# A four-layer graph network on one core: in the six SAGE rounds, a pair's gathered rows are transposed in front of the units of the pair ahead, and GpSimd scatters before it gathers

## The chip, the cores and the metric

The kernel runs on one core of one Trainium2 chip. The metric is the time on the device in microseconds. Of the kernel before there are three runs, and one more execution that was profiled.

## The reference

There are N = 100,000 nodes with 128 float32 features each and 50,000 edges (`src`, `dst`), sorted by `dst`. The destinations are drawn as the square of a uniform number, so they crowd at low node numbers: few nodes per edge at first, many later. Four layers follow each other, each with a residual and a layer norm.

```python
def _sage_conv(x, src, dst, W_l, b_l, W_r, n_nodes):           # layer 0, twice
    agg = jax.ops.segment_sum(x[src], dst, num_segments=n_nodes)
    cnt = jax.ops.segment_sum(jnp.ones((src.shape[0],), x.dtype), dst, num_segments=n_nodes)
    mean = agg / jnp.maximum(cnt, 1.0)[:, None]
    out = mean @ W_l + b_l + x @ W_r
    norm = jnp.linalg.norm(out, axis=-1, keepdims=True)
    return out / jnp.maximum(norm, 1e-12)                       # then relu
def sage_conv(h, W_l, W_r, bias):                               # layer 1, four times
    agg = jax.ops.segment_sum(h[src], dst, num_segments=n) * inv_deg[:, None]
    return jax.nn.relu(agg @ W_l + h @ W_r + bias)
...
x = _layernorm(x + _L0_gnn_ref(...), axis=-1)
x = _layernorm(x + _L1_gnn_ref(...), axis=-1)
x = _layernorm(x + _L2_gnn_ref(...), axis=-1)    # a graph attention layer
x = _layernorm(x + _L3_gnn_ref(...), axis=-1)    # a transformer layer with edge features
```

## The kernel before, in words

The kernel makes eight rounds over all edges and nodes and an output pass. Rounds 0 to 5 are SAGE rounds: rounds 0 and 1 are layer 0 (each with a division by the row's norm, round 1 with the residual and layer norm as well), rounds 2 to 5 are layer 1 (relu alone, round 5 with residual and layer norm). Round 6 is the attention layer (GAT), round 7 the transformer layer (TR). The change touches the SAGE rounds alone.

**Edges.** They are cut into 98 blocks of 512, and two blocks (q = 0 and 1) make a pair, so that a round has 49 pairs. For a block of a SAGE round:

- GpSimd gathers its source rows with 4 indirect DMAs of 128 rows each into `gath[q]` (`gathers`, L609), once DVE has put the block's source indices into `g_idx[q]` (`next_gather`, L1345, which waits until the last gathers with these indices have landed).
- PE transposes them into the bank `pe_bank[q]` (printed as edge_bank; L768) and raises `gt_ready[q]`.
- DVE runs one scan over 512 edges (L1363), which sums the rows of edges with one destination into `run[q]`, and copies the block's destination indices to `s_idx[q]` (`next_scatter`, L1351). The scan needs the last column of the scan before, so scans are serial.
- PE multiplies `run[q]` by W_l (L774) into `pe_bank[2 + q]`; ACT scales the rows by the inverse degree into `y_rows[q]` (L943) and raises `y_ready[q]`.
- GpSimd scatters y_rows with 4 indirect DMAs into `agg` in HBM (`scatters`, L618), where rows that are no end of a run go out of bounds and are left out.

**Nodes.** They are cut into 97 units of 1,024 (two groups s of 512) and a tail. For each unit SP loads the rows (`h_in`, L533) and the aggregates (`agg_in`, L539); PE transposes the rows (`front`, L856); ACT copies them to `h_t` (L1016); PE adds the bias (L862) and the product with W_r (L865) into `o_bank`; DVE adds the aggregates (`total`, L1521); ACT or DVE make relu or norms and ACT stores the rows. PE and ACT work one unit ahead (`front(u + 1)` in `unit(u)`).

**The order.** Each engine runs its own program in its own order, and semaphores tie them together. On PE, DVE, ACT and SP `schedule` sets it: for each pair i first `edge_pair(i)`, then the units whose last edges lie in the pairs before i. The number of units behind a pair comes from a table (`unit_end`) that the kernel works out from the edges: in a SAGE round 8 pairs have none, 11 have one, 13 have two, 11 three, 5 four, and behind the last pair come the remaining eight. SP waits ahead of the units of pair i for the scatters of the pairs before i. GpSimd has no units. Its loop of a SAGE round is the gathers of pair i+1 (both q), then the scatters of pair i (both q), with a wait in front of each. The attention and transformer rounds (`STAGGERED`) have another loop, which stays.

## Time and profile before

| | |
|---|---|
| median of 3 runs | 17478.66 us (17463.14 to 17509.43) |
| the profiled execution | 17477.8 us, its span 17476.0 us |
| rounds 0 to 5 (SAGE) | from about 1920 to 11900 us |
| attention round, transformer round | to about 14500, to about 16750 us |
| busy share of the span | PE 52%, DVE 42%, POOL 43%, ACT 29% |
| granted TensorE clock | 0.666 of 2.4 GHz, mean over the span |

The busy share is that of an engine over the whole span. In the rows further down, a time in front is the start in us from the span's start, the next number is how long the group of instructions was busy, and what stands in brackets at the end is the time for which that engine had been idle and what ended the wait: an instruction, a DMA, "issue" where nothing that the profile shows was waited for, or "remote" where the trace has no event near the end of the wait that could have released it. POOL is GpSimd, SPq and ACTq are the DMA issues of SP and ACT.

### The profile page before, as it was taken

What the parts mean: (1) busy time and instruction counts of PE and PEld (TensorE: products, weight loads), DVE (VectorE), ACT (ScalarE), POOL (GpSimd) and SP (SyncE); (2) the same over time, 40 slices, a digit from 0 to 9 for tenths busy, and PEclk for the clock granted to TensorE, in tenths of its full rate; (3) what the DMA queues carried; (4) which work ended last, traced back from release to release, by engine and by line L of the source; (5) the groups of instructions that cost most, each with busy time, mean ns of one, the idle gap of its engine ahead of it and who ended that gap; (6) DMA issues with size and microseconds to landing.
All of it is one profiled execution on the core that took longest, in us unless ns stands there. A gap on an engine that the chain in (4) does not pass through costs nothing. (4 is left out here: it accounts for less than half of the span.)

```text
span 17476.0 us, 215795 instructions
## 1 busy us (share of the span) xinstructions
PE 9144.7 (52%) x39289; PEld 6376.8 (36%) x39290; DVE 7406.0 (42%) x20909; ACT 5025.3 (29%) x11680; POOL 7457.3 (43%) x7460
## 2 busy tenths in 40 slices
PE   3664345534444455455545544554444446777765
PEld 1121234433333344344434434443333333444444
DVE  3664234424444112111111213446777774444456
ACT  0000022223443122122212213334555552222247
POOL 0546554354322654554365455433333326554410
PEclk9776566656665667666656765666666666677776
DMA  5000134524443245334424534554333332233457
GB/s 244 1 3 1 49 113 139 159 78 124 135 137 112 87 137 163 94 120 151 151 84 138 164 95 137 160 177 144 114 111 112 115 107 59 70 95 111 123 181 246
DMA packets 1168748, 2071.10 MB, mean 119 GB/s; under 512 B 283745, under 2 KB 292466, under 8 KB 1155794
## 3 DMA queue, kind: packets, MB, share of 16 engines
q1 hardware_dynamic: 662400, 1128.29, 21.5%
q10 hardware_dynamic: 267958, 563.32, 8.3%
q0 software_dynamic: 238336, 378.92, 8.0%
q14 instruction: 38, 0.31, 0.0%
q8 instruction: 16, 0.26, 0.0%
HBM read 1358.91 MB, written 772.63 MB: 122 GB/s over the span
## 5 line engine op out<-in xcount | busy, mean ns | idle before, releaser
L618 POOL DMA_INDIRECT agg<-y_rows,s_idx x3136 | 3229.8, 1030 | 2746.4 <-DVE s_idx L1351 1380.1
L862 PE MATMUL o_bank<-b_parts,ones_parts 3*128 3x512 bf16 (+1 forms) x1568 | 826.1, 527 | 4435.1 <-ACT h_t L1016 2314.9
L865 PE MATMUL o_bank<-w_r,h_t 128*128 128x128 f32 x12544 | 2804.2, 393 | 0.0
L865 PEld LDWEIGHTS o_bank<-w_r,h_t 128*128 128x128 f32 x12544 | 2394.9, 285 | 577.0 <-issue 576.1
L1521 DVE TENSOR_TENSOR total<-o_bank,agg_in 128x512 f32<-128x512 f32 (+1 forms) x1568 | 1042.7, 688 | 3353.4 <-DMA agg_in<-agg 2032.6
L609 POOL DMA_INDIRECT gath<-node_a,g_idx x1176 | 1130.7, 961 | 2414.4 <-DVE g_idx L1345 1174.7
L1016 ACT ACTIVATE h_t<-ht_bank 128x512 f32<-128x512 f32 (+1 forms) x1568 | 881.5, 593 | 3995.6 <-remote 2661.3
L862 PEld LDWEIGHTS o_bank<-b_parts,ones_parts 3*128 3x128 bf16 (+1 forms) x1568 | 150.4, 96 | 4816.2 <-ACT h_t L1016 2952.6
L609 POOL DMA_INDIRECT gath<-node_x,g_idx x784 | 785.6, 1002 | 1502.4 <-PE edge_bank L808 629.0
L943 ACT ACTIVATE y_rows<-edge_bank,inv 128x128 f32<-128x128 f32 x2352 | 671.5, 370 | 2609.7 <-remote 1039.6
L774 PE MATMUL edge_bank<-w_l,run 128*128 128x128 f32 x4704 | 903.3, 358 | 944.9 <-DVE run L1363 884.3
L1363 DVE TENSOR_TENSOR_SCAN run<-keep,run,edge_bank 128x512 f32<-128x512 f32 (+1 forms) x588 | 752.5, 1280 | 1201.9 <-PE edge_bank L768 570.2
L856 PE MATMUL ht_bank<-ident,h_in 128*128 128x128 f32 x6272 | 1125.2, 337 | 220.7 <-issue 113.2
L597 POOL DMA_INDIRECT rec_dram<-rec_rows,place_idx x784 | 755.4, 963 | 1121.4 <-DVE rec_rows L1302 896.5
L774 PEld LDWEIGHTS edge_bank<-w_l,run 128*128 128x128 f32 x4704 | 798.3, 259 | 1066.2 <-DVE run L1363 999.5
L1082 ACT ACTIVATE h_out<-t,small 128x128 f32<-128x128 f32 x2744 | 1102.6, 486 | 208.6 <-DVE small L1510 155.6
L609 POOL DMA_INDIRECT gath<-node_b,g_idx x784 | 786.2, 1003 | 799.7 <-PE edge_bank L768 414.3
L856 PEld LDWEIGHTS ht_bank<-ident,h_in 128*128 128x128 f32 x6272 | 976.2, 181 | 378.7 <-issue 282.0
L1526 DVE TENSOR_REDUCE small<-zeros 128x4 f32<-128x512 f32 x392 | 262.3, 684 | 1088.2 <-ACT zeros L1028 643.7
L768 PE MATMUL edge_bank<-ident,gath 128*128 128x128 f32 x2352 | 468.1, 359 | 460.7 <-DMA gath<-node_a,g_idx 216.1
L736 PE MATMUL edge_bank<-keep,rest_ones 128*128 128x512 bf16 (+1 forms) x784 | 336.1, 429 | 595.2 <-DVE place_f L1291 373.2
L609 POOL DMA_INDIRECT gath<-in_x_dram,g_idx x392 | 374.1, 954 | 634.8 <-DVE g_idx L1345 296.7
(249 smaller groups left out, 14550.0 us busy)
## 6 DMA issues: line engine op xcount, KB each, us to landing
agg_in<-agg SPq DMA_DIRECT2D x1560, 256.0 KB
node_a<-h_out ACTq DMA_DIRECT2D x780, 256.0 KB
h_in<-node_a SPq DMA_DIRECT2D x780, 256.0 KB
node_x<-h_out ACTq DMA_DIRECT2D x390, 256.0 KB
h_in<-node_x SPq DMA_DIRECT2D x390, 256.0 KB
node_b<-h_out ACTq DMA_DIRECT2D x390, 256.0 KB
h_in<-node_b SPq DMA_DIRECT2D x390, 256.0 KB
agg<-zeros ACTq DMA_DIRECT2D x96, 1024.0 KB
```

Source lines behind the costliest of these rows:

```text
L597: pool.indirect_dma_start(rec_dram[n], bass.IndirectOffsetOnAxis(place_idx[q][:, k:k + 1], 0), rec_rows[q][:, k, :], None).then_inc(rec_ou ...
L609: pool.indirect_dma_start(gath[q][:, k, :], None, h_of, bass.IndirectOffsetOnAxis(g_idx[q][:, k:k + 1], 0)).then_inc(gathered[q], 16)
L618: pool.indirect_dma_start(agg[order(r)], bass.IndirectOffsetOnAxis(s_idx[q][:, k:k + 1], 0), y_rows[q][:, k, :], None, bounds_check=N - 1, ...
L774: last = pe.matmul(pe_bank[2 + q][:, k * P:(k + 1) * P], run[q][:, k * P:(k + 1) * P], w_l[r][:], start=True, stop=True, skip_group_check= ...
L856: last = pe.transpose(ht_bank[s][:, j * P:j * P + p], h_in[s][0:p, j, :], ident[0:p, 0:p])
L862: pe.matmul(o_bank[s][0:p, :], ones_parts[:, 0:p], b_parts[:, r, :].unsqueeze(1).to_broadcast([3, RPP, P]), start=True, stop=False, skip_g ...
L865: last = pe.matmul(o_bank[s][0:p, j * P:(j + 1) * P], h_t[s][:, j, 0:p], w_r[r][:], start=False, stop=j == RPP - 1, skip_group_check=True)
L943: last = act.activation(y_rows[q][:, k, :], pe_bank[2 + q][:, k * P:(k + 1) * P], ACT.Copy, scale=inv[:, bass.ds(2 * i + q, 1), k])
L1016: act.activation(h_t[s][:, :, 0:p], ht_bank[s][:].rearrange("p (j n) -> p j n", j=RPP)[:, :, 0:p], ACT.Copy).then_inc(ht_ready[s], 1)
L1082: last = act.activation(h_out[s][0:p, j, :], of[s][0:p, j, :], ACT.Identity, scale=small2[0:p, 2 + 2 * turn, s * RPP + j:s * RPP + j + 1], ...
L1363: dve.tensor_tensor_scan(run[q][:], keep_of(i, q), pe_bank[q][:], run[1 - q][:, BLOCK - 1:BLOCK], ALU.mult, ALU.add).then_inc(run_ready[q], 1)
L1521: dve.tensor_tensor(flat(total[s], p), o_bank[s][0:p, :], flat(agg_in[s], p), ALU.add).then_inc(sum_ready[s], 1)
```

## The change

In the SAGE rounds three programs are written in another order.

- **PE.** The transposes of a pair (`sage_turn`) are taken out of `sage_pair`. Those of pair 0 come ahead of the schedule, behind `front(0)`; those of pair i+1 come right behind the W_l matmuls of pair i, so in front of the units of pair i.
- **DVE.** The copies of gather indices for the pair behind the next (`next_gather`) come behind both scans of pair i instead of in front of each, and wait for the gathers of pair i+1; two of them come ahead of the schedule.
- **GpSimd.** The gathers of two pairs come first; then the loop is scatters of pair i, gathers of pair i+2; the last two steps are scatters alone.

```diff
--- before.py
+++ after.py
@@ -645,23 +645,16 @@
                         for q in range(2):
                             next_scatters(q, n)
                     continue
-                with pool.Fori(0, PAIRS - 1) as i:
-
-                    for step, q in ((gathers, 0), (gathers, 1), (scatters, 0), (scatters, 1)):
-                        if step == gathers:
-
-                            pool.wait_ge(gt_ready[q], gt_ready.at(r, i + 1))
-                            pool.wait_ge(gidx_ready[q], gidx_ready.at(r, i + 2))
-                        else:
-
-                            pool.wait_ge(sidx_ready[q], sidx_ready.at(r, i + 1))
-                            pool.wait_ge(y_ready[q], y_ready.at(r, i + 1))
-                        pool.sem_inc(pool_turn, 1)
-                        step(q)
                 for q in range(2):
-                    pool.wait_ge(sidx_ready[q], sidx_ready.at(r, PAIRS))
-                    pool.wait_ge(y_ready[q], y_ready.at(r, PAIRS))
-                    scatters(q)
+                    next_gathers(q, 2)
+                with pool.Fori(0, PAIRS - 2) as i:
+                    for q in range(2):
+                        next_scatters(q, i + 1)
+                    for q in range(2):
+                        next_gathers(q, i + 3)
+                for n in (PAIRS - 1, PAIRS):
+                    for q in range(2):
+                        next_scatters(q, n)
 
 
         @block.tensor
@@ -760,13 +753,14 @@
             for r in range(NR):
                 kind, tail = ROUNDS[r][0:2]
 
+                def sage_turn(i, q, r=r):
+                    pe.wait_ge(gathered[q], gathered.at(r, i + 1))
+                    pe.wait_ge(run_ready[q], run_ready.at(r, i))
+                    for k in range(CPB):
+                        last = pe.transpose(pe_bank[q][:, k * P:(k + 1) * P], gath[q][:, k, :], ident[:])
+                    last.then_inc(gt_ready[q], 1)
+
                 def sage_pair(i, r=r):
-                    for q in range(2):
-                        pe.wait_ge(gathered[q], gathered.at(r, i + 1))
-                        pe.wait_ge(run_ready[q], run_ready.at(r, i))
-                        for k in range(CPB):
-                            last = pe.transpose(pe_bank[q][:, k * P:(k + 1) * P], gath[q][:, k, :], ident[:])
-                        last.then_inc(gt_ready[q], 1)
                     for q in range(2):
                         pe.wait_ge(run_ready[q], run_ready.at(r, i + 1))
                         pe.wait_ge(y_ready[q], y_ready.at(r, i))
@@ -774,6 +768,9 @@
                             last = pe.matmul(pe_bank[2 + q][:, k * P:(k + 1) * P], run[q][:, k * P:(k + 1) * P],
                                              w_l[r][:], start=True, stop=True, skip_group_check=True)
                         last.then_inc(yp_ready[q], 1)
+                    if not (isinstance(i, int) and i == PAIRS - 1):
+                        for q in range(2):
+                            sage_turn(i + 1, q)
 
 
 
@@ -888,6 +885,9 @@
                     tr_score(0, 0)
                     tr_values(0, 0)
                 front(0)
+                if kind == SAGE:
+                    for q in range(2):
+                        sage_turn(0, q)
                 schedule(pe, r, {SAGE: sage_pair, GAT: gat_pair, TR: tr_pair}[kind], lambda i: None, unit)
 
 
@@ -1356,13 +1356,15 @@
 
                 def sage_pair(i, r=r):
                     for q in range(2):
-                        next_gather(i, q, r)
                         dve.wait_ge(gt_ready[q], gt_ready.at(r, i + 1))
                         dve.wait_ge(yp_ready[q], yp_ready.at(r, i))
                         dve.wait_ge(run_ready[1 - q], run_ready.at(r, i + q))
                         dve.tensor_tensor_scan(run[q][:], keep_of(i, q), pe_bank[q][:], run[1 - q][:, BLOCK - 1:BLOCK],
                                                ALU.mult, ALU.add).then_inc(run_ready[q], 1)
                         next_scatter(i, q, r)
+                    if not (isinstance(i, int) and i == PAIRS - 1):
+                        for q in range(2):
+                            next_gather(i + 1, q, r)
 
                 def maxima(i, q, r, st, logits):
 
@@ -1583,6 +1585,9 @@
                             dve.bn_stats(place, ht_bank[s][:].rearrange("p (j n) -> p j n", j=RPP)[:, :, 0:p]).then_inc(bn_ready[s], 1)
                     st.end()
 
+                if kind == SAGE:
+                    for q in range(2):
+                        next_gather(0, q, r)
                 if kind == GAT:
                     gat_first()
                 if kind == TR:
```

PE, from the end of unit 0's front in round 0 to the head of its pair loop, before. `gath` are the gathered rows, `run` the scanned sums, and the load of `unit_end` is where the units of the pair begin:

```order
L865 MATMUL o_bank<-w_r,h_t 128x128 x4
L389 UNCONDITIONAL_BRANCH
L389 ISA
L768 MATMUL edge_bank<-ident,gath 128x128 x8
L771 REGISTER_ALU
L774 MATMUL edge_bank<-w_l,run 128x128 x8
L392 ISA
L392 TENSOR_LOAD unit_end
```

And the same stretch of the changed kernel:

```order
L862 MATMUL o_bank<-w_r,h_t 128x128 x4
L760 MATMUL edge_bank<-ident,gath 128x128 x8
L389 UNCONDITIONAL_BRANCH
L389 ISA
L766 REGISTER_ALU
L768 MATMUL edge_bank<-w_l,run 128x128 x8
L757 REGISTER_ALU
L760 MATMUL edge_bank<-ident,gath 128x128 x8
L392 ISA
L392 TENSOR_LOAD unit_end
```

The transposes with `gath` stood ahead of the matmuls with `w_l` in the loop; now they stand behind them, ahead of the units, and once in front of the loop.

GpSimd's loop of round 0 before, with the semaphores that each row waits for (`agg` is the table in HBM that is scattered to):

```order
L654 REGISTER_ALU [waits gt_ready0]
L609 DMA gath<-in_x_dram,g_idx 128x128 [waits gidx_ready0]
L609 DMA gath<-in_x_dram,g_idx 128x128 x3
L609 DMA gath<-in_x_dram,g_idx 128x128 [waits gt_ready1,gidx_ready1]
L609 DMA gath<-in_x_dram,g_idx 128x128 x3
L618 DMA agg<-y_rows,s_idx 100000x128 [waits sidx_ready0,y_ready0]
L618 DMA agg<-y_rows,s_idx 100000x128 x3
L618 DMA agg<-y_rows,s_idx 100000x128 [waits sidx_ready1,y_ready1]
L618 DMA agg<-y_rows,s_idx 100000x128 x3
L648 REGISTER_ALU
L648 COMPARE_AND_BRANCH
```

The same loop of the changed kernel:

```order
L618 DMA agg<-y_rows,s_idx 100000x128 [waits sidx_ready0,y_ready0]
L618 DMA agg<-y_rows,s_idx 100000x128 x3
L618 DMA agg<-y_rows,s_idx 100000x128 [waits sidx_ready1,y_ready1]
L618 DMA agg<-y_rows,s_idx 100000x128 x3
L622 REGISTER_ALU
L623 REGISTER_ALU [waits gt_ready0]
L609 DMA gath<-in_x_dram,g_idx 128x128 [waits gidx_ready0]
L609 DMA gath<-in_x_dram,g_idx 128x128 x3
L609 DMA gath<-in_x_dram,g_idx 128x128 [waits gt_ready1,gidx_ready1]
L609 DMA gath<-in_x_dram,g_idx 128x128 x3
L650 REGISTER_ALU
L650 COMPARE_AND_BRANCH
```

The gathers, which had their two waits for `gt_ready` at the head of the loop, now stand behind the scatters with their waits for `y_ready`. Since one pair more is gathered in front of the loop, the sequence of DMAs over the round is the same in both.

## Rows read from the trace of the kernel before

**Rows 1.** The head of the page: span, then busy time of each engine

```profile
span 17476.0 us, 215795 instructions
...
PE 9144.7 (52%) x39289; PEld 6376.8 (36%) x39290; DVE 7406.0 (42%) x20909; ACT 5025.3 (29%) x11680; POOL 7457.3 (43%) x7460
```

**Rows 2.** Windows of rounds 1 and 4: us, PE, PEld, DVE, ACT, POOL, PEclk

```profile
3520.00:5590.00 2070.00, 895.74 (x3724) 726.97 (x3724) 911.60 (x3138) 789.58 (x1960) 763.91 (x784) 0.60 0.39 120
...
8660.00:10190.00 1530.00, 763.33 (x3724) 610.16 (x3724) 284.48 (x492) 330.89 (x784) 762.65 (x784) 0.67 0.41 129
```

**Rows 3.** Windows of round 4 cut by pairs: pairs 0-10, 19-29, 40-47

```profile
8672.10:8910.90 238.80, 75.95 (x322) 62.07 (x322) 35.59 (x67) 29.36 (x92) 155.57 (x160) 0.56 0.17 49
...
9137.50:9470.90 333.40, 175.09 (x808) 140.41 (x809) 61.77 (x108) 72.01 (x172) 171.25 (x176) 0.64 0.42 132
...
9810.20:10127.00 316.80, 179.93 (x948) 141.86 (x946) 64.06 (x106) 83.81 (x180) 124.53 (x128) 0.73 0.54 169
```

**Rows 4.** Timeline of a pair of round 4: start, us, engine, line, [idle before]

```profile
9256.63 0.98 POOL L609 DMA_INDIRECT gath<-node_b,g_idx  x1 [12.88 <-PE edge_bank L768]
...
9265.67 0.60 ACT L1016 ACTIVATE h_t<-ht_bank 128x512 f32<-128x512 f32 x1 [3.22 <-remote]
...
9268.73 1.91 PE L856 MATMUL ht_bank<-ident,h_in 128*128 128x128 f32 x8
...
9272.69 3.51 SPq L539 DMA_DIRECT2D agg_in<-agg  x2
...
9275.79 0.98 POOL L618 DMA_INDIRECT agg<-y_rows,s_idx  x1 [0.30 <-issue]
9279.25 1.29 DVE L1521 TENSOR_TENSOR total<-o_bank,agg_in 128x512 f32<-128x512 f32 x2 [18.58 <-remote]
9279.31 1.09 ACT L1016 ACTIVATE h_t<-ht_bank 128x512 f32<-128x512 f32 x2 [12.00 <-remote]
...
9285.00 1.80 PE L768 MATMUL edge_bank<-ident,gath 128*128 128x128 f32 x8
9286.20 1.28 DVE L1363 TENSOR_TENSOR_SCAN run<-keep,run,edge_bank 128x512 f32<-128x512 f32 x1 [5.58 <-PE edge_bank L768]
9287.01 0.98 POOL L609 DMA_INDIRECT gath<-node_b,g_idx  x1 [10.24 <-PE edge_bank L768]
```

**Rows 5.** View of waits, 9150 to 10130: us in total, times, longest

```profile
ACT h_t L1016 <- remote: 427.5, 68, 17.0
```

**Rows 6.** Timeline of another pair of round 4, whose burst paused

```profile
9509.31 0.97 POOL L609 DMA_INDIRECT gath<-node_b,g_idx  x1 [2.05 <-issue]
...
9511.50 1.09 ACT L1016 ACTIVATE h_t<-ht_bank 128x512 f32<-128x512 f32 x2 [0.73 <-PE ht_bank L856]
...
9529.83 1.30 ACT L1016 ACTIVATE h_t<-ht_bank 128x512 f32<-128x512 f32 x2 [16.20 <-remote]
...
9533.82 0.97 SPq L539 DMA_DIRECT2D agg_in<-agg  x2
...
9535.43 1.19 PE L768 MATMUL edge_bank<-ident,gath 128*128 128x128 f32 x8
...
9537.13 0.98 POOL L609 DMA_INDIRECT gath<-node_b,g_idx  x1 [8.96 <-PE edge_bank L768]
```

**Rows 7.** Timeline in round 0, behind a burst that began with scatters

```profile
2190.20 2.18 ACT L943 ACTIVATE y_rows<-edge_bank,inv 128x128 f32<-128x128 f32 x8 [19.41 <-remote]
...
2192.26 1.02 POOL L618 DMA_INDIRECT agg<-y_rows,s_idx  x1 [4.38 <-issue]
```

**Rows 8.** Timeline of the last pair of round 4

```profile
10127.00 1.28 DVE L1363 TENSOR_TENSOR_SCAN run<-keep,run,edge_bank 128x512 f32<-128x512 uint8 x1 [3.62 <-PE edge_bank L768]
...
10128.34 1.16 PE L774 MATMUL edge_bank<-w_l,run 128*128 128x128 f32 x8 [0.94 <-DVE run L1363]
...
10131.54 0.98 POOL L618 DMA_INDIRECT agg<-y_rows,s_idx  x1 [25.79 <-ACT y_rows L943]
```

**Rows 9.** Timeline in round 1, the first gather of a burst

```profile
4262.63 0.98 POOL L609 DMA_INDIRECT gath<-node_a,g_idx  x1 [19.52 <-DVE g_idx L1345]
```

## The prediction

> **What bounds the kernel now.** I read the page's head first: over the span no engine is busy for more than 52% [rows 1], so the time is waits, and a view of one pair has to say which. The windows by round come next. A relu round of 1530 us holds 762.65 us of GpSimd DMAs, 784 of them [rows 2]; with the 0.30 us of issue between two of them [rows 4] that is 762.65 + 784 × 0.30 = 998 us, and PE and DVE have less. Then I cut that round by how many units follow a pair. The first eleven pairs have hardly a unit behind them and take 238.80 / 11 = 21.7 us each; eleven with mostly two units 333.40 / 11 = 30.3; the last eight before the end, with three or four, 316.80 / 8 = 39.6 [rows 3]. In the timeline of one pair with two units GpSimd's burst of 16 DMAs runs from 9256.63 to 9275.79 + 0.98 = 9276.77, 20.14 us, and the next burst starts at 9287.01 after 10.24 us of idleness [rows 4]. So the early pairs stand at GpSimd's floor of about 20.4 us (20.14 + 0.30), and the others pay the burst plus a serial piece behind it.
>
> Why is there a serial piece? The units could run beside the burst. In the timeline the unit's transposes L856 end at 9268.73 + 1.91 = 9270.64, but the h_t copy that waits for nothing else starts at 9279.31, 2.54 us behind the burst's end, 12.00 us of waiting put down to "remote"; DVE's sum at 9279.25 waited 18.58 us in the same way; SP's issue of two loads of agg in mid-burst takes 3.51 us [rows 4] where it takes 0.97 behind a burst [rows 6]. The view of waits gives 427.5 us of 980 to that h_t wait [rows 5]. So I take it as what this trace shows: many counts raised while a burst runs are seen only at its end or behind it. The pair's first units still get some through: an h_t copy 9 us into the burst waited 3.22 us, that of the next unit 12.00 [rows 4]. One unit's transposes, h_t and matmuls get into the burst, and the rest is done behind it.
>
> **The change, part by part.** *The order of DMAs on GpSimd does not change.* G0 G1 S0 G2 S1 G3 ... stands in both programs; only what releases a burst does. Before, [G(i+1) S(i)] starts when the transposes of pair i are done; now [S(i) G(i+2)] starts when ACT has written y_rows of pair i, and the gathers behind need only counts that came before. So 784 DMAs a round and 20.14 us a burst stay.
>
> *Term A, the burst starts later.* Before, from the first transpose to the first gather: 9287.01 − 9285.00 = 2.01 us, and at a second place 9537.13 − 9535.43 = 1.70 [rows 4, 6]; the middle is 1.85. Now the burst waits for w_l matmul, y_rows, scatter: a round's last pair has that path, since its gathers are over: 10131.54 − 10128.34 = 3.20 us [rows 8]. The transposes themselves (1.80 us, [rows 4]) leave this place, as the pair's scan finds them done, and the scan's 1.28 us now runs beside the last unit's matmuls. The price is 3.20 − 1.85 = +1.35 us for each pair that has units behind it. If the scan is the last to come, as it stands behind the sums on DVE, it is 10131.54 − 10127.00 = 4.54 from the scan on against 9287.01 − 9286.20 = 0.81: +3.73. Taken: +1.35; bounds 0 and +3.73.
>
> *Term B, units get a start over the burst.* The units of pair i stand behind w_l matmul and the moved transposes, and the burst starts 3.20 us after that matmul's start; before, the gathers had started the burst ahead of it. The moved transposes take 1.19 to 1.80 us of that lead on PE [rows 6, 4] and eat part of it. What a lead is worth the trace shows where a burst lost its second DMA by 2.05 us: from its second DMA at 9509.31 the rest of the pair is as if the burst had started some 2 us late. Both h_t copies at 9511.50 then are on time (0.73), the next unit's is late again (16.20 us), and GpSimd idles 8.96 us behind the burst where it idles 10.24 in the common one [rows 6, 4]. So 10.24 − 8.96 = 1.28 us come back. Taken: −1.28 for a pair with two units or more, 0 for a pair with one (its unit fits already); bounds 0 and −5 (half of the 10.24).
>
> A and B leave +0.07 us for a pair of two or more units and +1.35 for one with one. A round has 8 pairs without a unit, 11 with one, 29 with two to four (by the table of the program), and the last. 11 × 1.35 + 29 × 0.07 = +17 us a round.
>
> *Term C, early pairs.* With no unit between, a gather no longer waits for the transposes of its own burst's pair, and scatters landed in a burst's first half free y_rows and s_idx in its second. They can come down from 21.7 to 20.4, no lower: 11 × −1 = −11 us a round; bounds 0 and −14. Against it: a burst that starts with scatters exists already at the start of round 0, where their order has slipped, and behind it GpSimd idles 4.38 us, 20.14 + 4.38 = 24.5 in place of 20.4, with y_rows late by 19.41 [rows 7].
>
> *Term D, a round's end.* The last two steps are scatters alone. Pair 47's burst is 8 DMAs in place of 16, and its four units' counts are freed 10 us sooner. Taken −5 a round; bounds 0 and −10.
>
> *PE and DVE.* The moved transposes and index copies are the same instructions, no more. On PE the units of pair i now stand behind a wait for gathers of i+1, which were issued one burst earlier and have landed wherever GpSimd has been idle 10 us. Where it is not idle (early pairs), few units wait behind them.
>
> *By round.* The three relu rounds and round 0: 17 − 11 − 5 = +1 us each, +4. Round 1 is bound by DVE and ACT: 911.60 us of DVE in 2070 [rows 2], and before each burst GpSimd waits 19.52 us for the g_idx copy, which DVE reaches only behind its sums and norms, though the transposes were ready: one pair takes the burst and that wait, 20.14 + 19.52 = 39.66 us [rows 9]. There the burst is 19.5 us short of being the bound; moved +3.73 behind the scan it ends later but nobody waits for its end, and the first unit gets a lead of 3.7 us in which its counts are on time. I take −1 us for each of 40 pairs, −40; bounds ±1.5 × 49 = ±74. Round 5 has a norm too, a shorter one, and lies between the two kinds: −15, bounds ±60. GAT, TR and the output pass keep their code. Sum: +4 − 40 − 15 = −51 us. The profiled run took 17477.8, 1.8 us round its span of 17476.0 [rows 1] and 0.9 us below the median of the three: 17477.8 − 51 = 17426.8, with the 0.9 back **17428 us**.
>
> One rule speaks against my reading of the bursts. The Trainium skill, page "DMA: Bandwidth & Descriptors", section "SWDGE vs HWDGE vs iDMA", says that each DMA engine has separate queues for GpSimd's and for SP's and ACT's transfers and goes round between them, and that transfers issued by SP and ACT are immune to interference with GpSimd's descriptor writing. By it the loads of a unit would pass beside any burst and the units run inside it, as rival 1 has it. The trace disagrees here: two loads took 3.51 us in mid-burst and 0.97 outside [rows 4, 6].
>
> **The rivals.** *1. Late counts belong to bursts that start with gathers.* If a burst that starts with scatters lets counts through, and the units have their 3 us of lead too, most of the idle 10.24 us goes. At 3 us a pair: 29 × 6 × −3 = −522, to 16,956; at 5 us −870, to 16,609. For it: the lead and 12 us of waiting for a copy that takes 0.6. Against: the scatter-first burst of [rows 7] had y_rows 19.41 us late. Chance 0.17.
>
> *2. Slower: the path to the burst is longer and the lead is worth nothing.* The place is the end of a pair's last unit: scan, w_l matmul, y_rows, scatter. Price +1.35 us × 40 pairs × 6 rounds = +324, less C and D of 16 × 6 = 96: +228, to 17,707. It decides when the lead is eaten by the moved transposes (1.19 to 1.80 of 3.20 us), so that only one h_t copy is on time as before; in rounds 0, 1 and 5, where sums come late on DVE, 3.73 in place of 1.35 adds up to 2.38 × 40 × 3 = 286 more. Against: two idle times of 10.24 and 8.96. Chance 0.25.
>
> *3. Nothing.* The order of DMAs is the same and the serial piece behind the burst is unit work: A to D cancel within 52 us. I count apart from my forecast, which has a sign by round, 0.10.
>
> **How the numbers follow.** My forecast (the late counts stay, A and B nearly cancel) has 0.48, its own range by the bounds of the terms 17,260 to 17,560. 0.3% of this kernel is 52 us, about what a measurement can tell from no change, and −51 stands on that edge: of 0.48 I give 0.24 to faster, 0.15 to same, 0.09 to slower. With the rivals: faster 0.24 + 0.17 = 0.41; same 0.15 + 0.10 = 0.25; slower 0.09 + 0.25 = 0.34. The range takes in rival 2 up to its middle and the weaker part of rival 1: 17,060 to 17,760, with about 0.12 left below and 0.08 above.
>
> **What would show it.** In a pair of two units: transposes of i+1 right behind the w_l matmul; burst of 8 scatters, then 8 gathers, 20.1 us; the first scatter 3.2 us behind the matmul; h_t copies of the first unit on time, the second unit's 2.5 us behind the burst's end; GpSimd idle about 10.3 us; period 30.4. The three cuts of round 4 should read about 20.7, 30.4 and 39 us. Wrong: h_t on time inside the burst (rival 1), or idle 11.5 us and more (rival 2). Round 1's pair should be about 1 us shorter than 39.66; if it is longer, burst and norm chain collide. What I cannot see is what a scatter-first burst does to counts of PE in a round with steady units.

## The result and the profile after

The changed kernel takes 17012.28 us (median of 4, 16999.46 to 17040.24), the one before, run beside it, 17474.62 us (median of 4). The ratio is 0.9737, 95% interval 0.9722 to 0.9752: 462 us faster. That is outside the range given, just beyond its lower end, and near the figures of rival 1. It isn't the whole result: on chips 2, 4, 8 and 9, where most of the experiments ran, the same kernel before takes about 14,430 us, and there the change makes it 0.55% slower. Both have to be explained.

The head of the page after, and its row of the scatters (busy, mean ns, idle time before them and what ended it):

```profile
span 17012.5 us, 216341 instructions
...
PE 8904.1 (52%) x39289; PEld 6211.4 (37%) x39290; DVE 7391.0 (43%) x20909; ACT 4986.6 (29%) x11680; POOL 7444.3 (44%) x7460
...
L618 POOL DMA_INDIRECT agg<-y_rows,s_idx x3136 | 3232.4, 1031 | 5500.0 <-ACT y_rows L943 2534.5
```

The busy times are those of before to within 3% ([rows 1]), since nothing was removed. GpSimd now waits in front of scatters, for y_rows, no longer in front of gathers: of its pauses of over 1 us in round 4, 44 of 52 stood before a gather and together all were 546.2 us; after, 3 of 51 do, and all are 443.5 us. The difference of 102.7 us is nearly all of the gain of round 4, 103.4 us (below).

Windows of the changed kernel, from the first scan of a round to that of the next (rounds 0, 1, 4, 5, then all behind the SAGE rounds; columns as in [rows 2]):

```profile
1933.20:3524.50 1591.30, 777.06 (x3726) 630.88 (x3725) 597.59 (x1669) 343.62 (x882) 761.41 (x784) 0.64 0.40 124
3524.50:5540.60 2016.10, 804.93 (x3728) 657.46 (x3726) 904.95 (x3139) 783.63 (x1960) 763.63 (x785) 0.62 0.40 123
...
8416.30:9845.20 1428.90, 743.77 (x3728) 598.57 (x3726) 285.64 (x493) 327.17 (x784) 761.31 (x785) 0.66 0.45 138
9845.20:11381.10 1535.90, 721.77 (x3494) 583.65 (x3492) 604.77 (x1998) 516.37 (x1367) 755.62 (x767) 0.63 0.49 150
11381.10:17012.50 5631.40, 3373.25 (x13134) 2159.82 (x13134) 3468.22 (x8986) 2356.82 (x5105) 2115.77 (x1968) 0.67 0.39 121
```

The window of round 5 ends with the first scan of its last pair. Cut in the same way the kernel before has 1595.9, 2070.7, 1532.3 and 1635.5 us for these rounds and 5636.1 for the rest. So round 4 gained 103.4 us (rounds 2 and 3 gained 93.2 and 101.9), round 5 99.6, round 1 54.6, round 0 4.6, and the rest 4.7. The first three relu rounds, of which I had said "+1 us each", bring 298.5 of the 462.

The same three stretches of round 4 as in [rows 3]:

```profile
8416.30:8641.00 224.70, 75.99 (x306) 59.78 (x305) 36.26 (x67) 28.71 (x92) 148.48 (x154) 0.55 0.17 47
...
8856.60:9162.60 306.00, 161.82 (x813) 130.46 (x811) 63.78 (x109) 71.31 (x172) 180.06 (x186) 0.67 0.47 143
...
9484.60:9770.90 286.30, 180.56 (x950) 145.20 (x950) 62.63 (x107) 81.52 (x180) 116.68 (x120) 0.71 0.59 187
```

From 238.80, 333.40 and 316.80 us to 224.70, 306.00 and 286.30. I had divided the first by eleven. That was a miscount: the row has 160 DMAs, ten pairs of 16, so the early pairs stood at 23.9 us, not at 21.7, and were not yet at GpSimd's floor; now they take 22.5. The pairs with mostly two units went from 30.3 to 27.8 us, the last eight from 39.6 to 35.8.

One pair with two units in the timeline of the changed kernel, from the W_l matmuls of one pair to the first scatter of the next (columns as in [rows 4]):

```profile
9062.56 2.53 PE L768 MATMUL edge_bank<-w_l,run 128*128 128x128 f32 x16
...
9064.93 1.04 PE L760 MATMUL edge_bank<-ident,gath 128*128 128x128 f32 x8
...
9066.50 1.02 POOL L618 DMA_INDIRECT agg<-y_rows,s_idx  x1 [5.42 <-issue]
9067.10 1.08 ACT L1016 ACTIVATE h_t<-ht_bank 128x512 f32<-128x512 f32 x2 [0.49 <-issue]
...
9073.14 1.47 PE L853 MATMUL ht_bank<-ident,h_in 128*128 128x128 f32 x8
...
9076.86 0.98 POOL L609 DMA_INDIRECT gath<-node_b,g_idx  x1 [0.31 <-issue]
9077.20 0.69 DVE L1523 TENSOR_TENSOR total<-o_bank,agg_in 128x512 f32<-128x512 f32 x1 [3.21 <-remote]
9078.02 1.28 DVE L1362 TENSOR_TENSOR_SCAN run<-keep,run,edge_bank 128x512 f32<-128x512 f32 x1
...
9080.10 0.60 ACT L1016 ACTIVATE h_t<-ht_bank 128x512 f32<-128x512 f32 x1 [9.44 <-remote]
...
9088.43 0.60 ACT L1016 ACTIVATE h_t<-ht_bank 128x512 f32<-128x512 f32 x1 [7.73 <-remote]
...
9091.48 3.39 PE L768 MATMUL edge_bank<-w_l,run 128*128 128x128 f32 x16
...
9095.70 1.02 POOL L618 DMA_INDIRECT agg<-y_rows,s_idx  x1 [9.09 <-issue]
```

The steps stand as predicted up to the burst's start: transposes of i+1 (9064.93) right behind the W_l matmul, 8 scatters, 8 gathers, the unit's first h_t copy on time at 9067.10. Then comes what the forecast did not have. The unit's sum and the scan of pair i+1 are done inside the burst, at 9077.20 and 9078.02, where before they came behind it ([rows 4]: 9279.25, 9286.20), and one more h_t copy runs 13.60 us into the burst (9080.10 − 9066.50). Of the units only one group's h_t and its matmuls are left behind the burst. GpSimd then idles 9.09 us here, 5.42 in the pair ahead. Counted over the records of pairs 19 to 39 of round 4, the idle time behind a full burst of 16 is 11.85 us before (19 bursts) and 8.93 us after (16).

The view of waits of round 4, 8900 to 9770 us (870 us long; that of [rows 5] is 980):

```profile
ACT h_t L1016 <- remote: 397.6, 57, 16.3
...
POOL agg L618 <- ACT y_rows L943: 212.1, 15, 17.1
...
DVE total L1523 <- remote: 145.7, 25, 15.3
```

The late h_t copies are still there, in total and at longest ([rows 5]: 427.5 and 17.0), so the counts raised inside a burst did not come on time. Which counts are late can be read more closely.

I set the end of each of PE's instructions that raise a count beside the time at which the trace has the count's update, in the full bursts of pairs 19 to 39 of round 4 (20 before, 17 after), by when they were raised. A count for which the trace has no update of its own is left out (10 before, 19 after):

| raised, us from the burst's start | before: number, share over 1 us late, mean delay | after |
|---|---|---|
| −2 to 2 | 70, none | 76, none |
| 2 to 4 | 18, 0.11, 0.2 us | 8, 0.25, 0.4 us |
| 4 to 6 | 38, 0.84, 5.3 us | 27, all, 6.8 us |
| 6 to 22 | 75, all | 57, all |

The limit is about the same in both orders: nearly all are prompt up to 2 us and all late from 6 us on, with the change at about 4 us (between 2 and 4 us after, 8 counts are few, and 4 more have no update of their own). What has changed is which counts fall ahead of it. For the counts of the units alone, from 4 us ahead of a burst to 22.5 us into it:

| count of | over time (1 us) | before, per burst | after, per burst |
|---|---|---|---|
| unit's transposes | prompt | 0.30 (6 of 72) | 1.82 (31 of 72) |
| | late, seen before the 20th us | 1.55 | 1.41 |
| | late, seen behind it | 1.75 | 1.00 |
| unit's matmuls | prompt | 1.35 | 0.71 |
| | late, seen before the 20th us | 0.05 | 1.06 |
| | late, seen behind it | 1.95 | 1.35 |

In round 2 it is the same (transposes prompt 8 of 110, then 52 of 119). Before, the first unit's transposes ended 4.7 to 5.1 us into the burst, just behind the limit; now they end by about its first half microsecond, and the chain of that unit is two steps on when counts begin to be late. In the attention round of the same trace of before, whose bursts go 4 scatters, 4 gathers, 4 scatters, 4 gathers, none of PE's 287 counts raised from 0 to 18 us (those with an update of their own) is late; of the 123 raised from 18 to 22.5 us, 118 are, by 2.8 us in the mean. So the attention round has late counts too, only much later in its burst.

### The profile page after: what moved, and what is told of

Its sections match the earlier page's. It is cut to its first block and busy times, and to the rows that moved or that the text cites. A ratio compares the mean times of both kernels' runs of the same rounds, so it can differ in the third digit from the quotient of the medians.

```text
span 17012.5 us, 216341 instructions
## 1 busy us (share of the span) xinstructions
PE 8904.1 (52%) x39289; PEld 6211.4 (37%) x39290; DVE 7391.0 (43%) x20909; ACT 4986.6 (29%) x11680; POOL 7444.3 (44%) x7460
## 5 line engine op out<-in xcount | busy, mean ns | idle before, releaser
L862 PE MATMUL o_bank<-w_r,h_t 128*128 128x128 f32 x12544 | 2636.0, 375 | 0.0
L862 PEld LDWEIGHTS o_bank<-w_r,h_t 128*128 128x128 f32 x12544 | 2248.1, 269 | 546.1 <-issue 545.5
L768 PE MATMUL edge_bank<-w_l,run 128*128 128x128 f32 x4704 | 954.5, 382 | 818.1 <-DVE run L1362 666.4
L768 PEld LDWEIGHTS edge_bank<-w_l,run 128*128 128x128 f32 x4704 | 890.1, 289 | 878.0 <-issue 791.1
L853 PE MATMUL ht_bank<-ident,h_in 128*128 128x128 f32 x6272 | 1059.1, 323 | 191.5 <-issue 84.8
L853 PEld LDWEIGHTS ht_bank<-ident,h_in 128*128 128x128 f32 x6272 | 910.5, 171 | 352.3 <-issue 254.5
L760 PEld LDWEIGHTS edge_bank<-ident,gath 128*128 128x128 f32 x2352 | 366.0, 184 | 1124.8 <-DMA gath<-node_a,g_idx 452.6
L1345 DVE COPY g_idx<-idx 128x8 int32 (+1 forms) x784 | 123.6, 173 | 1466.7 <-DMA gath<-node_a,g_idx 569.7
```

What stands on the lines that cost most here:

```text
L760: last = pe.transpose(pe_bank[q][:, k * P:(k + 1) * P], gath[q][:, k, :], ident[:])
L768: last = pe.matmul(pe_bank[2 + q][:, k * P:(k + 1) * P], run[q][:, k * P:(k + 1) * P], w_l[r][:], start=True, stop=True, skip_group_check= ...
L853: last = pe.transpose(ht_bank[s][:, j * P:j * P + p], h_in[s][0:p, j, :], ident[0:p, 0:p])
L862: last = pe.matmul(o_bank[s][0:p, j * P:(j + 1) * P], h_t[s][:, j, 0:p], w_r[r][:], start=False, stop=j == RPP - 1, skip_group_check=True)
```

## The experiments

The kernel before, run beside them, has two kinds of time: about 14,430 us on chips 2, 4, 8 and 9, and 17,726 us on chip 0, near the 17,475 us of the first measurement. Chip 9 was met twice, the others once, so it isn't shown that the chip makes the difference and not something else between these measurements. Ratios are to the kernel before on the same chip, run beside. The changed kernel as it stands was not run on chip 0.

### Where counts are on time: the two kernels themselves

**before_again**, the kernel before, and **after_again**, the changed kernel, both unaltered.

> The kernel before itself, for its trace in the place where the experiments run. Theory A: if it takes about 14,430 us, counts raised during a burst of GpSimd's DMAs are on time in its trace (delay under 1 us) and its SAGE rounds are bound by GpSimd in most pairs; if it takes about 17,475, they are late as in the first trace. Rival (the places differ in the speed of engines or DMAs): the same late counts, but shorter instructions or DMAs.

> The changed kernel itself, unaltered. The kernel before took 17,475 us in the runs beside the change's first measurement and 14,432 us in the runs beside the first four experiments. Theory A (late counts are a condition of the first place, and the change gains only where they are late): if before runs at about 17,475 here, the ratio is 0.974 again; if it runs at about 14,430, the ratio is 1.000 to 1.006. Rival (the change gains in the same proportion anywhere): 0.974 in both cases.

Measured: before 14,427.9 us (one execution, chip 8); after 14,523.78 us, ratio 1.0055 (1.0035 to 1.0075, chip 2). In both traces none of PE's counts in a burst is over 1 us late, and the same holds for the SAGE rounds in all 16 traces of chips 2, 4, 8 and 9. Late counts are in the traces of the first measurement and of chip 0 (block_before: 40 of 331 counts raised inside bursts of the SAGE rounds, 167 of 473 in the attention round). A pair of round 4 in before_again:

```profile
7461.50 0.69 DVE L1521 TENSOR_TENSOR total<-o_bank,agg_in 128x512 f32<-128x512 f32 x1 [0.34 <-DMA agg_in<-agg]
...
7462.94 1.08 ACT L1016 ACTIVATE h_t<-ht_bank 128x512 f32<-128x512 f32 x2 [0.72 <-PE ht_bank L856]
...
7467.03 1.08 ACT L1016 ACTIVATE h_t<-ht_bank 128x512 f32<-128x512 f32 x2 [1.96 <-PE ht_bank L856]
...
7469.55 1.02 POOL L618 DMA_INDIRECT agg<-y_rows,s_idx  x1 [0.30 <-issue]
...
7475.37 1.68 PE L768 MATMUL edge_bank<-ident,gath 128*128 128x128 f32 x8
...
7476.57 1.28 DVE L1363 TENSOR_TENSOR_SCAN run<-keep,run,edge_bank 128x512 f32<-128x512 f32 x1 [4.70 <-PE edge_bank L768]
...
7479.93 0.98 POOL L609 DMA_INDIRECT gath<-node_b,g_idx  x1 [0.30 <-issue]
```

Both h_t copies of the units run inside the burst, after 0.72 and 1.96 us from the transposes; the transposes of the next pair (7475.37) are done before the burst's last scatters, and the next gathers start at 7479.93, 0.30 us behind them. There is no serial piece behind this burst; the one before it began after 3.32 us of idleness, and in round 4 GpSimd's pauses of over 1 us are 20 with 129.3 us, against 52 with 546.2 in the first trace. GpSimd's DMAs are as long as in the first trace (gather 0.95, scatter 0.98 us), so what differs isn't their speed but when counts arrive. PE's granted clock is higher too (0.79 in round 4 against 0.67), but its busy time there is only 85 us less, where the round is 409 us shorter. Windows by round (0, 1, 4, the rest) of before_again:

```profile
1647.40:2821.70 1174.30, 710.43 (x3724) 571.68 (x3724) 602.07 (x1669) 347.02 (x882) 767.30 (x786) 0.76 0.52 168
2821.70:4554.70 1733.00, 843.01 (x3724) 691.31 (x3724) 909.62 (x3139) 785.41 (x1960) 761.88 (x784) 0.64 0.46 143
...
6820.20:7943.10 1122.90, 678.21 (x3724) 542.59 (x3724) 291.54 (x492) 333.59 (x784) 761.56 (x783) 0.79 0.55 176
...
9120.90:14426.00 5305.10, 3233.94 (x13138) 2061.79 (x13136) 3470.77 (x8987) 2357.12 (x5098) 2114.66 (x1968) 0.70 0.41 129
```

and of after_again:

```profile
1648.60:2853.90 1205.30, 751.37 (x3728) 605.50 (x3726) 598.23 (x1669) 343.01 (x882) 762.68 (x785) 0.69 0.52 164
2853.90:4609.60 1755.70, 799.73 (x3724) 651.78 (x3723) 904.68 (x3139) 784.35 (x1960) 762.92 (x785) 0.63 0.45 142
...
6884.40:8011.50 1127.10, 680.43 (x3726) 537.77 (x3724) 285.49 (x493) 333.65 (x784) 761.43 (x785) 0.75 0.55 175
...
9186.70:14529.60 5342.90, 3265.35 (x13134) 2078.39 (x13134) 3467.03 (x8986) 2360.06 (x5105) 2114.95 (x1968) 0.69 0.41 128
```

Round 4 is 1122.9 and 1127.1 us, of which GpSimd's 784 DMAs with their issue take 998, so 125 us at most could be gained; the pauses stay as they were (129.3 and 130.7 us). Rounds 0 and 1 lose 31.0 and 22.7 us, their pauses grow from 173.2 and 742.1 to 211.1 and 763.7 us. I take it that the later start of a burst lengthens the chain over their norms on DVE and ACT; that wasn't tested by itself. Theory A stands, the rival (the same proportion anywhere) falls. Of the 3,050 us between the traces of the kernel before in the first measurement and on chip 8, 287 lie ahead of round 0, 2,432 in the SAGE rounds and 331 behind them; that all of it comes from late counts isn't shown.

**mixed** keeps the order of before in rounds 0 and 1 (PE and DVE), the changed one in 2 to 5.

```diff
+    AHEAD = (2, 3, 4, 5)
...
                 def sage_pair(i, r=r):
+                    if r not in AHEAD:
+                        for q in range(2):
+                            sage_turn(i, q)
...
-                    if not (isinstance(i, int) and i == PAIRS - 1):
+                    if r in AHEAD and not (isinstance(i, int) and i == PAIRS - 1):
```

> The changed order on PE and DVE in rounds 2 to 5 only; rounds 0 and 1 keep the order of before. From the traces of both kernels where before takes 14,430: rounds 0 and 1 are 31 and 23 us longer in the changed kernel, rounds 2 to 5 together 11 us. Theory (what is lost is lost in the rounds with norms): 1.001 of before, at most 1.003. Rival (it is spread over the relu rounds and the run to run difference hides it): 1.004 or more. Where before takes about 17,500: 0.977, since rounds 0 and 1 gave 59 of the 462 us there.

Measured: 14,433.69 against 14,410.95 us (chip 4), ratio 1.0016 (1.0006 to 1.0025). Most of the 0.55% sat in rounds 0 and 1, which take 1168.6 and 1736.1 us here, as in the kernel before. It does not beat the kernel before there, and where counts are late it wasn't measured.

### Parts of the change, where counts are on time

**e_pool_loop_old** puts GpSimd's loop of before into the changed kernel.

> The changed kernel with GpSimd's loop of before (gathers of pair i+1, then scatters of pair i); PE and DVE as changed. GpSimd's sequence of DMAs and the counts each waits for are the same in both, only the place of the loop's branch differs. Theory A (the whole gain comes from where PE and DVE raise their counts): 17,012 us within 50. Rival (the form of the loop matters, its branch and waits fall elsewhere in a burst): over 17,100.

Measured: ratio 1.0052 (1.0035 to 1.0068, chip 9), beside 1.0055 for the changed kernel on chip 2. The expectation's 17,012 was for the other kind of chip; as a ratio the two are the same. GpSimd's part of the diff does nothing where counts are on time, as the order listing says: the same DMAs with the same waits.

**e_pe_old** undoes PE's part, **e_dve_old** DVE's (each with the instructions that stand ahead of the schedule as well).

```diff
                 def sage_pair(i, r=r):
+                    for q in range(2):
+                        sage_turn(i, q)
...
-                    if not (isinstance(i, int) and i == PAIRS - 1):
-                        for q in range(2):
-                            sage_turn(i + 1, q)
```

```diff
                     for q in range(2):
+                        next_gather(i, q, r)
                         dve.wait_ge(gt_ready[q], gt_ready.at(r, i + 1))
...
-                    if not (isinstance(i, int) and i == PAIRS - 1):
-                        for q in range(2):
-                            next_gather(i + 1, q, r)
```

> The changed kernel with PE's order of before (transposes of a pair at its head, behind the units of the pair ahead); DVE and GpSimd as changed. Gathers of pair i+2 wait for transposes of pair i+1, so the burst is scatters, a pause over the units, gathers. Theory A (the moved transposes are what allows one unbroken run of DMAs behind y_rows): GpSimd is held up in mid-burst and the time is over that of before by 1% or more where it takes 17,475, by 3% or more where it takes 14,430. Rival (the index copies and scatters first do it): as the changed kernel, within 0.5%.

> The changed kernel with DVE's order of before (index copies in front of each scan); PE and GpSimd as changed. Gathers of pair i+2 are released only at the head of pair i+1, and the transposes of pair i+2 stand in front of the units of pair i+1, so these units wait some 12 us for the gathers. Theory A: slower than before by 10% or more (12 us x 40 pairs x 6 rounds = 2,900 us less what of it was idle time). Rival (index copies are free to stand anywhere): as the changed kernel within 0.5%.

Measured on chip 2: 1.0796 (1.0774 to 1.0819) and 1.0873 (1.0851 to 1.0895), the second with 8.7% where I expected 10% or more. Each half alone is far worse than neither. In e_pe_old GpSimd's gathers wait for the transposes (222.1 us in 26 waits, the longest 18.4, from 6850 to 7900 us). In e_dve_old they wait for the index copies (208.5 us in 26 waits) and PE's transposes for the gathers (184.8 us in 54), with the units behind them. The change is one thing in two parts.

**e_gathers_first** swaps the halves of the burst, **e_stagger** takes the attention round's order, **e_throttle** keeps GpSimd from running more than 8 DMAs ahead.

```diff
                     for q in range(2):
+                        next_gathers(q, i + 3)
+                    for q in range(2):
                         next_scatters(q, i + 1)
-                    for q in range(2):
-                        next_gathers(q, i + 3)
```

```diff
-    STAGGERED = (GAT, TR,)
+    STAGGERED = (GAT, TR, SAGE)
```

```diff
                     for q in range(2):
+                        pool.wait_ge(scattered[q], scattered.at(r, i + 1))
                         next_gathers(q, i + 3)
```

> The changed kernel with a burst of gathers of pair i+2, then scatters of pair i, both released behind the W_l matmul of pair i. Lead theory: burst begins at about the same time behind that matmul, so 17,012 within 80. Order theory (a burst that begins with scatters lets counts through at the change to gathers): most of the gain of 462 us is lost, over 17,250.

> The changed kernel with GpSimd's order scatters q0, gathers q0, scatters q1, gathers q1 in SAGE rounds, as the attention round has it. Lead theory (counts are late from the fourth microsecond of any unbroken run of 16 DMAs, and the units gain by being ahead of it): the same order of run, 17,012 within 60. Order theory (runs of four of each kind let counts through, as in the attention round, where counts of PE were on time up to the 18th microsecond of a burst): under 16,750.

> The changed kernel; GpSimd waits in front of the gathers of each q until its scatters of the same q have landed (they were issued 5 us earlier, so the wait should be over before its turn), which keeps its sequencer from running more than 8 DMAs ahead. Run-ahead theory (counts are late when many DMAs stand issued ahead in GpSimd's queue): counts on time in more of the burst, under 16,800. Lead theory and order theory: no effect but the wait's own cost, 17,012 to 17,080.

Measured: 1.0337 (1.032 to 1.0355), 1.0082 (1.0066 to 1.0099) and 1.0053 (1.0037 to 1.007), all on chip 9. They were meant to tell how late counts are let through, and ran where none is late, so they decide nothing on that. They do show that scatters in front matter by themselves: with the gathers in front the kernel takes 14,919.34 us against 14,500.40 for e_pool_loop_old beside it, 2.9% more. In its trace the longest wait is that of ACT's y_rows copies for landed scatters (444.1 us in 66 waits, 6850 to 7900 us), and DVE's copies to s_idx wait 403.9 us for the same; neither is among the seven longest in e_pool_loop_old.

**e_before_late** gives the kernel before nothing but the start of the units over the burst.

```diff
                             pool.wait_ge(gt_ready[q], gt_ready.at(r, i + 1))
+                            if q == 0:
+                                pool.wait_ge(y_ready[1], y_ready.at(r, i + 1))
```

> The kernel before with one wait more: the first gathers of a burst wait for y_rows of the same pair, so that the burst begins 3 to 4 us later behind the scan, as in the changed kernel, while transposes and scan stay behind the units. It gives the units the start over the burst and nothing else. Lead theory (the start over the burst alone is worth more than the 3.7 us that it costs, where counts are late): faster than before by 100 to 300 us at 17,475. Rival (the gain comes from transposes and scan leaving the path behind the units): slower by 3.7 - 1.3 = 2.4 us x 40 x 6 = 580 us at most, 200 at least. Where before takes 14,430, with few late counts: slower by over 500 us by both.

Measured on chip 2: 1.0513 (1.0493 to 1.0533), 736.65 us, or 736.65 / 288 = 2.6 us for each of 48 × 6 bursts: where GpSimd has little idle time, a burst that starts later costs most of its delay. As expected for this kind of chip, and again silent on the other.

### The path behind the units, where before takes 17,726 us

**block_before** and **block_after** hold PE's units until the burst beside them has landed, so that neither has work beside a burst and neither has a start over it. In the kernel before the units wait for `scattered`, in the changed one for `gathered`, the last DMAs of the burst:

```diff
+                def pe_block(i, r=r):
+                    for q in range(2):
+                        pe.wait_ge(scattered[q], scattered.at(r, min(i + 1, PAIRS) if isinstance(i, int) else i + 1))
-                schedule(pe, r, {SAGE: sage_pair, GAT: gat_pair, TR: tr_pair}[kind], lambda i: None, unit)
+                schedule(pe, r, {SAGE: sage_pair, GAT: gat_pair, TR: tr_pair}[kind],
+                         pe_block if kind == SAGE else lambda i: None, unit)
```

> The kernel before with PE's units (and all that PE does behind them) held until the scatters of the same pair have landed, that is until the whole burst [gathers of i+1, scatters of i] is over, in every pair of the SAGE rounds. It puts by a wait what late counts do in the first trace: no unit work beside the burst. Alone it gives the scale: about 48 x 6 x 5 us = 1,400 us slower than a before of 14,430; smaller than that against a before of 17,475. Its worth is the difference to its partner.

> The changed kernel with PE's units held in the same way until its whole burst [scatters of i, gathers of i+2] has landed. Neither of the two has a start of units over the burst; they differ in what stands behind the units. Term A as I had it (from the last unit to the first DMA of the next burst 3.20 us instead of 1.85): slower than block_before by 1.35 x 48 x 6 = 390 us; with the scan late on DVE, 3.73 in place of 1.35, up to 1,070 us. Rival (transposes and scan leave the path behind the units, which is where the measured gain comes from): faster than block_before, by 200 to 500 us.

Measured on chip 0: 19,365.84 us (ratio 1.0928, 1.091 to 1.0946) and 20,285.21 us (1.1443, 1.1424 to 1.1462): with no unit work beside a burst the changed order is 919 us slower, where with it, in the first measurement, it is 462 us faster. So the gain comes from what the units do beside bursts, provided that the change gains on chip 0 too, which was not measured. The rival, that the moved scan and transposes shorten the path, falls. The end of a pair in block_before (last scatter, first transposes of the held units, last matmuls of the last unit, transposes, first gather):

```profile
9802.54 0.98 POOL L618 DMA_INDIRECT agg<-y_rows,s_idx  x1 [0.30 <-issue]
...
9806.92 1.94 PE L856 MATMUL ht_bank<-ident,h_in 128*128 128x128 f32 x8 [20.32 <-issue]
...
9823.36 2.08 PE L865 MATMUL o_bank<-w_r,h_t 128*128 128x128 f32 x8
...
9825.23 1.91 PE L768 MATMUL edge_bank<-ident,gath 128*128 128x128 f32 x8
...
9827.23 0.98 POOL L609 DMA_INDIRECT gath<-node_a,g_idx  x1 [23.70 <-PE edge_bank L768]
```

and in block_after (last gather, units' transposes, scan, last matmuls, W_l matmuls, first scatter):

```profile
9823.79 0.94 POOL L634 DMA_INDIRECT gath<-node_a,g_idx  x1 [0.30 <-issue]
...
9828.38 1.94 PE L878 MATMUL ht_bank<-ident,h_in 128*128 128x128 f32 x8 [23.73 <-issue]
...
9837.40 1.28 DVE L1389 TENSOR_TENSOR_SCAN run<-keep,run,edge_bank 128x512 f32<-128x512 f32 x1 [0.35 <-issue]
...
9838.15 1.16 PE L887 MATMUL o_bank<-w_r,h_t 128*128 128x128 f32 x8
...
9839.14 2.28 PE L793 MATMUL edge_bank<-w_l,run 128*128 128x128 f32 x16
...
9842.48 1.02 POOL L643 DMA_INDIRECT agg<-y_rows,s_idx  x1 [17.75 <-ACT y_rows L970]
```

From the end of the units' last matmul to the burst: 9827.23 − 9825.44 = 1.79 us against 9842.48 − 9839.31 = 3.17 us, a difference of 1.38, as term A had it (1.35). The units start 4.38 and 4.59 us behind the start of the last DMA. Over whole rounds more is lost: by first scans the relu rounds take 1824.0, 1822.6, 1819.1 before and 1934.6, 1914.6, 1932.8 after, together 316 us or 2.2 us a pair; rounds 0 and 1 take 1889.9 and 2499.6 before, 2092.0 and 2733.0 after, 4.2 and 4.9 us a pair, nearer to the bound of 3.73 for a scan that comes last on DVE; round 5 takes 2006.3 and 2171.4, 3.4 us a pair.

Most of the other 0.8 us in the relu rounds is that the pair shown isn't the usual one: over its 1.79 us the granted clock was 0.50 (1.2 GHz), over its 3.17 us 1.00. Taken over all bursts of the relu rounds that begin less than 12 us behind the end of a unit's last matmul, that distance has the median 1.39 us in block_before (119 bursts) and 3.33 in block_after (116), a difference of 1.9. In the first measurement, with nothing held, it is 1.79 us before (115 bursts) and 3.89 after (86): 2.1 us, where term A had 1.35.

### The repeats

**e_stagger_b**, **before_late_b**, **before_late_c**, **gathers_first_b**, **gathers_first_c** and **throttle_b** are the kernels of those names again ("e_" left out in some), one execution each, meant for a chip with late counts.

> Scatters q0, gathers q0, scatters q1, gathers q1 again, for one look beside the kernel before. If before takes about 17,475: lead theory 0.974 of before, order theory under 0.96. If before takes about 14,430: 1.008 as measured before.

> The kernel before whose burst waits for y_rows of its pair, once more. Where before takes about 17,500 (late counts): if the start of the units over the burst is the cause, faster than before by 100 to 600 us although the burst begins 3.7 us later; if order or the moved scan is the cause, slower by 200 us or more. Where before takes about 14,430: 1.05 of before, as measured.

> As for before_late_b: where before takes about 17,500, faster than before by 100 to 600 us if the start over the burst is the cause, slower by 200 us or more if not; 1.05 where it takes 14,430.

> The changed kernel with gathers of i+2 in front of scatters of i, once more. Where before takes about 17,500: if the start over the burst is the cause, ratio to before 0.97 to 0.985 (its burst begins at about the same time behind the W_l matmul); if scatters in front are the cause, 1.00 or more. Where before takes about 14,430: 1.034, as measured.

> As for gathers_first_b: where before takes about 17,500, 0.97 to 0.985 of it if the start over the burst is the cause, 1.00 or more if the scatters in front are; 1.034 where it takes 14,430.

> The changed kernel whose gathers wait for landed scatters of the same q, once more. Where before takes about 17,500: run-ahead theory (counts are late when many DMAs stand issued ahead) under 0.96 of before; lead and order theory 0.974 as the changed kernel. Where before takes about 14,430: 1.005, as measured.

All ran on the other kind. With the kernel before at 14,433 us (chips 8 and 9) and 14,411 (chip 4), e_stagger_b took 14,573 us (chip 8), before_late 15,163 (chip 9) and 15,164 (chip 4), gathers_first 14,910 (chip 9) and 14,915 (chip 4), throttle_b 14,514 (chip 9). They repeat the first figures (the three of before_late and of gathers_first each within 0.1%) and leave the question open.

## Why the prediction was wrong

*What bounds the kernel.* Right where the trace was taken. "Many counts raised while a burst runs are seen only at its end or behind it" is what both traces show, yet it isn't a property of the program: on chips 2, 4, 8 and 9 no count is late and the program runs 17% shorter.

*The order of DMAs.* Right: e_pool_loop_old equals the changed kernel where counts are on time.

*Term A, "the burst starts later", +1.35 us.* Its place was right, its size too small: 2.1 us between the medians of the two traces of the first measurement, 2.2 with the units held (4.2 and 4.9 in rounds 0 and 1, where the bound of 3.73 was the better value). The 3.20 us came from a round's last pair, over which the granted clock was 1.00 (2.4 GHz); over the two old paths it was 0.61 and 0.91, and over the two that the timeline of the changed kernel shows 0.80 and 0.64. So the new path was read from a place where PE was faster than in most pairs, and the 1.85 us of the old one contain matmuls at 1.2 GHz. Alone this error would have made the kernel slower than forecast.

*Term B, "units get a start over the burst", −1.28 us: the step that failed.* In relu rounds 2 to 4 the change brought 298.5 / 144 = 2.1 us a pair, in spite of term A's 2.2. So B, C and D together are about −4.3 us a pair, where 1.28 for 29 of 48 pairs, C's 11 and D's 5 us made 53 / 48 = 1.1. This takes the terms as additive; even with term A at nothing, 2.1 us a pair are left, nearly twice the 1.1. The bound of −5 that I had written beside B would have held it, but my range did not use it: 3.72 us more for 29 pairs in four rounds are 431 us, which gives 16,997, and so "by the bounds of the terms" the forecast's own range should have reached at least there instead of ending at 17,260. I had priced the lead from one burst that had paused 2.05 us, by what GpSimd idled behind it. That burst still had the pair's scan and transposes behind it. The 0 for a pair with one unit had the same fault: before, that unit's transposes ended 4.7 to 5.1 us into the burst, and most of their counts were late. In the changed kernel the scan and one or two groups of a unit more are done within the burst, and so the GpSimd idle time fell by 2.92 us (11.85 to 8.93) even though term A is contained in it. The table of counts shows the lead at work (the unit's transposes' counts are prompt in 1.82 cases a burst instead of 0.30), and the kernels with held units point to work beside the burst as the place of the gain; that the lead alone does it is argued, not shown. What part the scatters in front have stays open: the kernels that separate the two never ran where counts are late.

*Term C.* −1.4 us a pair (23.9 to 22.5) for ten pairs, −14 us in round 4, as the bound had it; but from a base that I had miscounted, so that the floor wasn't near. *Term D.* From the first scan of the last pair of round 4 to the first of round 5, 77.4 us became 74.3: −3 of the −5. But this end was one of the better ones: from the last scan of a round to the first of the next, the ends of rounds 0 to 4 changed by +2.1, +4.0, +2.1, −3.0 and −3.1 us, so the term is nothing in the mean.

*By round.* "−40" for round 1 was near (−54.6), but its −1 us a pair was read from no row. "+1" for round 0 was near too (−4.6), by luck: there the path to the burst grew by 4.2 us a pair with the units held, and B, C and D took as much back. "−15" for round 5 was far off (−99.6), and the relu rounds worst.

*The rivals.* Rival 1 gave the time (16,956 for 3 us a pair) but not by its mechanism: counts raised behind the 4th us of a burst that starts with scatters are as late as before; those of the first unit's transposes are simply raised in time. Rival 2's place was real and its price of +1.35 us even too low, as block_after shows; the lead outweighed it. Where counts are on time, rival 3, nothing, is nearest for the relu rounds (1122.9 and 1127.1), and the whole is 0.55% slower.

*The rule set against this reading.* The section "SWDGE vs HWDGE vs iDMA" of the Trainium skill's page "DMA: Bandwidth & Descriptors" says that GpSimd's and SP's and ACT's transfers stand in different queues of a DMA engine, which takes them in turn. I had read more into it, that the units would run inside the burst, and called the first trace a disagreement, for SP's issue of two loads took 3.51 us in mid-burst. That is the time of an issue and not of a transfer, and the section says nothing of it or of PE's counts. On chips 2 and 8 nothing in the traces speaks against it: units run beside bursts, and the issue of two loads of agg more than 4 us into a burst has from 5000 to 9000 us the median 0.96 and 0.93 us (265 and 273 cases), against 3.50 in the first trace (18 cases). Neither it nor a run here tells why PE's counts are late elsewhere.

## What to carry to other kernels

Before a serial piece is priced, ask whether it is a property of the program or of the chip on which the trace was taken: here the relu rounds of one program have two bounds, GpSimd's DMAs on four chips and late counts in the first measurement and on chip 0, and one change has opposite signs. A price that is the difference of two rows should be read where the granted clock is the same, and from the median of many pairs rather than from one. Where signals are late in a part of a cycle, count which signals each order raises ahead of that part, rather than how long the pieces of the cycle are. And parts of a reordering that hold each other up (transposes and index copies) are measured together: alone they cost 8.0% and 8.7%.

## What the runs showed of the hardware

- The same kernel takes 17,475 us in the first measurement and 17,726 us on chip 0, and 14,411 to 14,441 us on chips 2, 4, 8 and 9, with single DMAs of the same length (0.95 and 0.98 us). In the SAGE rounds of the 16 traces of chips 2, 4, 8 and 9 no count of PE raised in a burst is over 1 us late.
- Where counts are late, it begins some 4 us into a burst of 16 indirect DMAs in SAGE rounds, whichever kind stands first, and half (after) to two thirds (before) of the late ones are seen 22 us from its start, some 2 us behind its end; in the attention round of the same trace none of 287 is late up to 18 us, and 118 of 123 from there on.
- SP's issue of two loads stretches there as well: from 5000 to 9000 us of the first trace the median is 3.50 us more than 4 us into a burst (18 cases) and 0.92 us elsewhere (218).
